# Three moves in the expert stage of a state-space and mixture-of-experts layer: a down product, a block of transposes and the weight loads

## The chip, the cores and the metric

The kernel runs on one core of a Trainium2 chip. The metric is the device time of one execution in microseconds. The core has a matrix engine (TensorE, PE in the profile), a vector engine (VectorE, DVE), an activation engine (ScalarE, ACT), a general engine (GpSimd, POOL) and a queue engine that only issues DMAs here (SyncE, SP). All five run their own instruction streams and meet by semaphores.

## What is computed

A layer with two halves, all in float32. Cut to what matters:

```python
# x: 2 x 1024 tokens of 512
x = x + mamba(layernorm(x))            # projection, conv, selective scan over 1024 steps, gate, projection
h = layernorm(x)
flat = rmsnorm(h) * norm_w             # 2048 x 512
scores = softmax(flat @ router_w.T)    # 32 experts
topk_w, topk_ids = top_k(scores, 4);  topk_w /= sum(topk_w)
for each expert e, its tokens xs:      # 8192 token-expert pairs, ragged
    g, u = split(xs @ w1[e])           # 512 -> 256 + 256
    ys   = (silu(g) * u) @ w2[e]       # 256 -> 512
    routed[token] += topk_w * ys
shared = (silu(flat @ sg) * (flat @ su)) @ sd
out = x + h + routed + shared
```

## The kernel before

It has two blocks of instruction streams, one behind the other; all engines pass from the first to the second together.

The first block (`front`) holds the state-space half, and a closing part with the norms, the router and the shared expert. In the closing the shared expert's down product of a tile of 128 tokens (`dn`, L1510, eight matmul records a tile) goes into one of two banks in turn, and DVE adds the bank to the tile's `base` (`add`, L1024); SP stores it. So the product of tile 14 needs the bank that the addition of tile 12 sets free. The last four tiles, 12 to 15, come at the very end. On DVE the rows of the first expert unit are turned between the last multiplication and the additions of tiles 12 to 15 (L1270 to L1274). The gathers of the first four slots (two units) were issued by POOL as soon as the slot list was known (L1406).

The second block (`experts`) works through units. A slot is 128 rows gathered for one expert; a unit is the two slots of one expert, or a single mixed slot that three experts share (the third unit in each of the first five groups of five). There are 37 units (`NU`), 25 in groups of five and 12 behind them, and 69 slots. The weights of four experts lie in a ring (`RING`), each "place" with 1 MB of gate and up weights (`w1r`) and 0.5 MB of down weights (`w2r`). For a unit u:

- POOL gathers its rows (`gather`, L1686), into one of three row buffers, once the unit three before it is turned; it scatters the finished rows into the output with an addition (`scatter`, L1699). Scatters of one expert are a batch; a batch may be issued only when the batch before it has landed (L1702). In POOL's stream the gather of unit u+4 stands ahead of the scatters of unit u.
- DVE turns the rows into `xT` (`rows_turned`, L1809; one of two buffers; 16 transposes, L171), takes the shares (`shares_of`), and multiplies silu(gate) by up (`mult`, L1815). Its stream is turned(u+2), mult(u+1), turned(u+3), ...
- PE makes the gate product (`gate`, L1897), the up product (`up`, L1907) and the down product (`down`, L1922) in the order gate(u+1), up(u+1), down(u).
- ACT applies silu to the gate product (`silu_gate`, L1768) and copies the down product, weighted with the share, to `y` (`weighted`, L1782, L1787).
- SP loads the next expert's weights into a place (L1664 to L1671): both loads once the last down product that reads the place is done (`y_done`). The gate product waits until both have landed (L1884).

Semaphore `xT_ready` counts the units turned in this block, all but the first; gathers and gate products wait for it by unit number.

Of the kernel before, what the change touches and what calls it, by code (L numbers as in the profile page):

```python
# [44 lines left out]
RING = 4  # L45
# [9 lines left out]
EARLY = 4  # L55
# [48 lines left out]
def front(nc, c, dram):  # L104

    ctx = ExitStack()
    with ctx:
# [93 lines left out]
        order_i, place = inside("order_i", [P, E], I32), inside("place", [P, E])  # L201
# [209 lines left out]
        with nc.Block(no_gpsimd_drain=True) as block:  # L411
# [461 lines left out]
            def _(eng):  # L873
# [390 lines left out]
                for u in range(1, UNITS):  # L1264
# [2 lines left out]
                            add(i)  # L1267
                    mult(u)
                    route(u - 1)
                for v in (0, 1):  # L1270
                    eng.wait_ge(c.gathered[v], 16)
                c.turned(eng, 0, 2)
                for i in range(UNITS - HC, UNITS):
                    add(i)  # L1274

# [281 lines left out]
def experts(nc, c, dram):  # L1557

    ctx = ExitStack()
    with ctx:  # L1560
# [34 lines left out]
        def last_slot(place):  # L1595

            m, v = divmod(place, RING)
            return m * SLOTS + (1, MIXED, 6, 8)[v] if m < SHARED else JOINT + 2 * (place - SHARED * RING) + 1
# [12 lines left out]

        NU = SHARED * (RING + 1) + E - SHARED * RING

        def single(u):
            return len(slots_of(u)) == 1

# [12 lines left out]
        def rows_landed(eng, u):  # L1629

            for n, b, v in row_buffers(u):
                eng.wait_ge(gathered[2 * b + v], 16 * sum(v < len(slots_of(w)) for w in range(b, u + 1, AHEAD // 2)))
# [17 lines left out]
        def after(eng, sem, value):  # L1650
            if value > 0:
                eng.wait_ge(sem, value)
# [9 lines left out]
        with nc.Block(no_gpsimd_drain=True) as block:  # L1662
            @block.sync
            def _(eng):  # L1664
                for place in range(RING, E):
                    u = place % RING
                    at = eng.value_load(c.expert_at[0:1, place:place + 1], min_val=0, max_val=E - 1)
                    ds = bass.ds(at, 1)
                    eng.wait_ge(S["y_done"], last_slot(place - RING) + 1)
                    eng.dma_start(c.w1r[:, u], dram.w1[ds].rearrange("a p k n -> (a p) k n")).then_inc(c.w_landed[u], 16)  # L1670
                    eng.dma_start(c.w2r[:, u], dram.w2[ds].rearrange("a p k n -> (a p) k n")).then_inc(c.w_landed[u], 16)  # L1671

                def one_more(r):
                    eng.wait_ge(S["y_done"], MAIN)
                    eng.wait_ge(R["y_done"], r + 1)
                    for v in range(2):
                        ds = bass.ds(eng.value_load(c.rest_at[0:1, bass.ds(r * 2 + v, 1)], min_val=0, max_val=E - 1), 1)
                        eng.dma_start(c.w1r[:, v], dram.w1[ds].rearrange("a p k n -> (a p) k n")).then_inc(R["w_landed"], 16)
                        eng.dma_start(c.w2r[:, v], dram.w2[ds].rearrange("a p k n -> (a p) k n")).then_inc(R["w_landed"], 16)
                rest(eng, one_more)  # L1680

            @block.gpsimd
            def _(eng):
                eng.sem_inc(R["sent"], 1)

                def gather(u):  # L1686

                    if u >= NU:
                        return
                    if u >= AHEAD // 2:  # L1690
                        old = u - AHEAD // 2
                        after(eng, S["xT_ready"], old)
                        eng.wait_ge(S["share_ready"], shares(last_of(old)))
                    for n, b, v in row_buffers(u):
                        eng.indirect_dma_start(out=xg[:, b, v, :], out_offset=None, in_=dram.flat,  # L1695
                                               in_offset=bass.IndirectOffsetOnAxis(ap=c.slot_token[:, n:n + 1], axis=0))\
                            .then_inc(gathered[2 * b + v], 16)
# [49 lines left out]
                def one_more(r):  # L1747
                    all_landed(eng)
                    eng.wait_ge(R["which_ready"], r * 2 + 2)
                    eng.wait_ge(S["xT_ready"], NU - 1)  # L1750
                    eng.wait_ge(S["share_ready"], shares(MAIN - 1))
                    passed(r, 0)
                    eng.indirect_dma_start(out=xg[:, 0, 0, :], out_offset=None, in_=dram.flat,
                                           in_offset=bass.IndirectOffsetOnAxis(ap=which[:, 0:1], axis=0)).then_inc(R["gathered"], 16)
                    eng.wait_ge(R["y_ready"], r + 1)
                    for v in range(2):
                        at = (which, into_upper)[v][0:PART, 0:1]
                        passed(r, 1 + v)
                        eng.indirect_dma_start(out=dram.out_rows, out_offset=bass.IndirectOffsetOnAxis(ap=at, axis=0),
                                               in_=y[halves[v], 0, :], in_offset=None, compute_op=ALU.add).then_inc(R["added"], 16)  # L1760
                        eng.wait_ge(R["added"], r * 32 + 16 * (v + 1))
                    passed(r, 3)
# [4 lines left out]
            def _(eng):  # L1767
# [14 lines left out]
                def weighted(n):  # L1782
                    eng.wait_ge(S["y_done"], n + 1)
                    eng.wait_ge(S["share_ready"], shares(n))
                    if n >= KEPT:
                        landed(eng, batch_of(n - KEPT))
                    eng.activation(y[:, n % KEPT, :], y_ps[n % 2][:], ACT.Copy, scale=share[:, n % SHARES:n % SHARES + 1])\  # L1787
                        .then_inc(S["y_ready"], 1)

                silu_gate(0)  # L1790
                for u in range(NU):
                    if u + 1 < NU:
                        silu_gate(u + 1)
                    if single(u):
                        act_turned(u)
                    for n in slots_of(u):
                        weighted(n)

                def one_more(r):
                    eng.wait_ge(R["h_done"], r + 1)  # L1800
# [7 lines left out]
            def _(eng):  # L1808
                def rows_turned(u):  # L1809
                    after(eng, S["up_done"], u - 1)  # L1810
                    rows_landed(eng, u)
                    c.turned(eng, u, len(slots_of(u))).then_inc(S["xT_ready"], 1)
                    shares_of(u)
# [18 lines left out]
                            eng.tensor_scalar(to[part, :], xg[part, b, v, bass.ds(at + (DM - 1), 1)], 0.0, None, ALU.add)\  # L1832
                                .then_inc(S["share_ready"], 1)

                rows_landed(eng, 0)
                shares_of(0)
                rows_turned(1)
                mult(0)
                for u in range(NU):
                    if u + 2 < NU:  # L1840
# [25 lines left out]
            def _(eng):  # L1866
# [15 lines left out]
                def ready_for(u):  # L1882
                    for place in places(slots_of(u)[0]):
                        eng.wait_ge(c.w_landed[place % RING], 32 * (place // RING + 1))  # L1884
                    after(eng, S["xT_ready"], u)
                    after(eng, S["act_ready"], u - 1)

                def inner(u, out, first):
# [49 lines left out]

                gate(0)
                up(0)  # L1940
                for u in range(NU):
                    if u + 1 < NU:
                        gate(u + 1)
                    if single(u):
                        turn_act(u)
                    if u + 1 < NU:
                        up(u + 1)
                    down(u)

                def one_more(r):  # L1950
                    eng.wait_ge(R["xT_ready"], r + 1)
# [95 lines left out]
```

## Time and profile before

| | us |
|---|---|
| three runs | 1613.62, 1617.28, 1618.94 |
| their median | 1617.28 |
| the profiled execution, time | 1620.9 |
| its span | 1618.9 |
| PE busy, share of the span | 1449.8, 90% |
| DVE busy | 1308.3, 81% |
| POOL busy | 1077.6, 67% |
| ACT busy | 741.5, 46% |

The expert block begins at about 1231 us and takes the last 388 us. PE is busy all through it, with a granted clock at full rate but for short stretches. The profile is read here by its views: the page (its parts are busy time, slices, queues, the chain that ended last, groups of instructions and DMA issues), the waits (who waited for whom), the timeline of each engine (start, duration, line, operation, output and inputs, count, and in brackets the idle time before and what ended it), and windows (busy time of each engine, granted clock and DMA share in a stretch). Times are from the start of the span.

### The profile page before, as it was taken

The numbers are of one execution on the slowest core, as the hardware profiler recorded it, in microseconds if no ns is written. First come the engines' busy times: TensorE is split into PE (matmuls) and PEld (weight loads), VectorE is DVE, ScalarE is ACT, GpSimd is POOL, SyncE is SP. The second block draws the span as 40 slices with busy tenths as digits, with TensorE's granted clock in tenths as the row PEclk, the third lists the DMA queues.
The fourth block names the chain that finished last, engine by engine and source line by source line (L and its number), as shares of the span: only waits on it lengthen the run. The fifth ranks groups of instructions, "written<-read, shape, count | busy, mean of one in ns | idle before, by whom it ended". The sixth has DMA issues, their size and how long they took to land. (4 is left out here: it accounts for less than half of the span.)

```text
span 1618.9 us, 14732 instructions
## 1 busy us (share of the span) xinstructions
PE 1449.8 (90%) x4412; PEld 725.0 (45%) x4413; DVE 1308.3 (81%) x1931; ACT 741.5 (46%) x1160; POOL 1077.6 (67%) x545
## 2 busy tenths in 40 slices
PE   6578998889998889998798878899998999999996
PEld 3233443334443334443343323444445766667774
DVE  4599999999999999999999997355636777777772
ACT  4566665776656776657566664421000111111111
POOL 0199898999887999989999997230011455555453
PEclk9889999899999999999899999999999999999998
DMA  4540112410113411103310004021412888888895
GB/s 131 221 174 9 42 48 101 179 40 30 35 47 108 171 41 36 35 15 126 129 36 21 28 1 156 20 104 33 182 54 64 225 237 225 218 239 223 259 260 68
DMA packets 63823, 176.86 MB, mean 109 GB/s; under 512 B 10304, under 2 KB 15168, under 8 KB 55040
## 3 DMA queue, kind: packets, MB, share of 16 engines
q1 hardware_dynamic: 48128, 138.59, 24.8%
q0 software_dynamic: 15616, 37.32, 11.1%
q8 instruction: 37, 0.61, 0.2%
q14 instruction: 42, 0.34, 0.1%
HBM read 142.98 MB, written 32.85 MB: 109 GB/s over the span
## 5 line engine op out<-in xcount | busy, mean ns | idle before, releaser
L1342 POOL TENSOR_TENSOR h<-h,c_rep 128x2048 f32<-128x2048 f32 x128 | 579.3, 4530 | 31.2 <-DVE h L945 26.1
L1542 PE MATMUL bank<-h,ident 128*128 128x512 f32 x916 | 449.3, 634 | 93.0 <-POOL h L1342 74.2
L717 ACT ACTIVATE bank<-delta,a_neg 128x512 f32<-128x512 f32 x512 | 335.8, 682 | 178.9 <-DVE h L945 178.1
L1542 PEld LDWEIGHTS bank<-h,ident 128*128 128x128 f32 x916 | 180.6, 202 | 335.9 <-issue 210.9
L945 DVE TENSOR_TENSOR_SCAN h<-bank,state,h 128x512 f32<-128x512 f32 x256 | 306.0, 1260 | 0.5 <-ACT bank L717 0.5
L945 DVE TENSOR_TENSOR_SCAN h<-bank,h 128x512 f32<-128x512 f32 x256 | 290.7, 1199 | 2.8 <-ACT bank L717 2.6
L171 DVE STREAM_TRANSPOSE xT<-xg 32x256 f32<-32x256 f32 (+1 forms) x592 | 247.3, 418 | 56.0 <-DMA xg<-flat,slot_token 48.3
L935 DVE TENSOR_TENSOR h<-bank,b_rep 128x2048 f32<-128x2048 f32 (+1 forms) x105 | 227.5, 2184 | 35.7 <-ACT bank L708 24.2
L1703 POOL DMA_INDIRECT out<-y,slot_token x64 | 101.8, 1590 | 110.1 <-DMA out<-y,slot_token 65.2
L1329 POOL TENSOR_TENSOR h<-du,b_rep 128x2048 f32<-128x2048 f32 (+1 forms) x32 | 125.4, 3920 | 11.5 <-PE bank L1542 11.5
L1787 ACT ACTIVATE y<-y_ps,share 128x512 f32<-128x512 f32 x69 | 47.4, 687 | 185.3 <-PE y_ps L1935 152.3
L1439 PE MATMUL bank<-xnT,w_in 128*128 128x512 f32 x256 | 120.4, 616 | 10.1 <-ACT zs L680 9.2
L1893 PE MATMUL g_ps<-xT,w_ring 128*128 128x256 f32 x512 | 119.4, 387 | 8.2 <-issue 4.3
L1471 PE MATMUL bank<-xnT,w_res 128*128 128x512 f32 x256 | 118.6, 607 | 0.1
L1461 PE MATMUL bank<-w_out,xs 128*128 128x512 f32 x256 | 115.6, 594 | 1.5 <-DVE xs L955 0.9
L1893 PEld LDWEIGHTS g_ps<-xT,w_ring 128*128 128x128 f32 x512 | 98.9, 194 | 38.1 <-issue 25.6
L1893 PE MATMUL u_ps<-xT,w_ring 128*128 128x256 f32 x512 | 115.7, 379 | 0.0
L1935 PE MATMUL y_ps<-w_ring,act 128*128 128x512 f32 x256 | 115.4, 594 | 0.0
L1893 PEld LDWEIGHTS u_ps<-xT,w_ring 128*128 128x128 f32 x512 | 96.9, 190 | 13.0
L1695 POOL DMA_INDIRECT xg<-flat,slot_token x65 | 64.9, 998 | 50.9 <-POOLq L411 25.6
L1407 POOL DMA_INDIRECT xg<-flat,slot_token x4 | 4.0, 1012 | 135.4 <-DVE slot_token L1210 134.5
L1439 PEld LDWEIGHTS bank<-xnT,w_in 128*128 128x128 f32 x256 | 49.9, 197 | 76.6 <-issue 62.4
(238 smaller groups left out, 1530.0 us busy)
## 6 DMA issues: line engine op xcount, KB each, us to landing
w_ring<-in_w SPq DMA_DIRECT2D x32, 1024.0 KB, 5.3
b_rep<-bcd SPq DMA_DIRECT2D x16, 1024.0 KB, 6.9
c_rep<-bcd SPq DMA_DIRECT2D x16, 1024.0 KB, 5.0
w_ring<-in_w SPq DMA_DIRECT2D x32, 512.0 KB, 7.4
w_in<-in_w_in_x SPq DMA_DIRECT2D x32, 256.0 KB, 2.6
w_res<-in_w_in_res SPq DMA_DIRECT2D x32, 256.0 KB, 2.6
xa<-in_x SPq DMA_DIRECT2D x20, 256.0 KB, 3.0
xb<-in_x SPq DMA_DIRECT2D x16, 256.0 KB, 3.0
```

The lines of the kernel that those rows point to most:

```text
L171: ins = eng.transpose(out[cols:cols + PIECE, 0:slots, :, rows:rows + PIECE], x[rows:rows + PIECE, :, :, cols:cols + PIECE])
L717: eng.activation(da[j][:], delta[:, g % 2], ACT.Exp, scale=a_neg[:, col:col + 1])\
L935: eng.tensor_tensor(h[:, q, a:b], du_ps[:].unsqueeze(1).to_broadcast([P, b - a, SEG]), b_rep[:, Q * q + a:Q * q + b, :], ALU.mult).then_in ...
L945: eng.tensor_tensor_scan(h[:, q, j, :], da[j][:], h[:, q, j, :], init, ALU.mult, ALU.add)\
L1329: eng.tensor_tensor(h[:, q, a:b], du[:].unsqueeze(1).to_broadcast([P, b - a, SEG]), b_rep[:, Q * q + a:Q * q + b, :], ALU.mult).then_inc(S ...
L1342: ins = eng.tensor_tensor(h[:, q], h[:, q], c_rep[:, Q * q:Q * q + Q, :], ALU.mult)
L1439: ins = eng.matmul(out[:], w_in[:, n % 2, k, :], xnT[:, s % 2, k, :], start=(k == 0), stop=(k == KC - 1))
L1461: eng.matmul(out[:], xs[:, s % 2, d, i * P:(i + 1) * P], w_out[:, d, :], start=(d == 0), stop=False)
L1471: ins = eng.matmul(out[:], w_res[:, i % 2, k, :], xnT[:, s % 2, k, :], start=(k == 0), stop=(k == KC - 1))
L1542: ins = eng.matmul(y_ps[:], c.ident[:], h[:, q, j, :], start=False, stop=(q == NQ - 1 and j == Q - 1))
L1893: ins = eng.matmul(out[:, f * 2 * P:(f + 1) * 2 * P], c.w1r[:, own, k, first + f * P:first + (f + 1) * P], xT[:, u % 2, k, :], start=(k == ...
L1935: ins = eng.matmul(y_ps[i][:], turned[:, k, v * P:(v + 1) * P], c.w2r[:, places(n)[0] % RING, k, :], start=(k == 0), stop=(k == FC - 1))
```

## The change

Three moves, with no instruction more or less:

1. DVE turns the rows of the second unit in the closing too, behind those of the first and ahead of the additions of tiles 12 to 15. In the expert block it only takes that unit's shares. `xT_ready` counts one unit fewer, so every wait for it asks for one less.
2. SP's load of the gate and up weights of a place waits for the up product of the unit that last used the place, and no longer for its down product. The load of the down weights waits as before and now stands behind it on SP.
3. The last but one unit's down product comes ahead of the last unit's gate product on PE, and on ACT the last unit's silu comes behind the weighted copies of the unit before it.

```diff
@@ front, vector engine, closing
-                for v in (0, 1):
-                    eng.wait_ge(c.gathered[v], 16)
-                c.turned(eng, 0, 2)
+                for u in (0, 1):
+                    for v in (0, 1):
+                        eng.wait_ge(c.gathered[2 * u + v], 16)
+                    c.turned(eng, u, 2)
                 for i in range(UNITS - HC, UNITS):
                     add(i)
@@ experts
+        def unit_of(n):
+            return next(u for u in range(NU) if n in slots_of(u))
@@ sync engine
+                    eng.wait_ge(S["up_done"], unit_of(last_slot(place - RING)) + 1)
+                    eng.dma_start(c.w1r[:, u], dram.w1[ds].rearrange("a p k n -> (a p) k n")).then_inc(c.w_landed[u], 16)
                     eng.wait_ge(S["y_done"], last_slot(place - RING) + 1)
-                    eng.dma_start(c.w1r[:, u], dram.w1[ds].rearrange("a p k n -> (a p) k n")).then_inc(c.w_landed[u], 16)
                     eng.dma_start(c.w2r[:, u], dram.w2[ds].rearrange("a p k n -> (a p) k n")).then_inc(c.w_landed[u], 16)
@@ gpsimd, gather
-                        after(eng, S["xT_ready"], old)
+                        after(eng, S["xT_ready"], old - 1)
@@ scalar engine
-                    if u + 1 < NU:
+                    if u < NU - 2:
                         silu_gate(u + 1)
                     if single(u):
                         act_turned(u)
                     for n in slots_of(u):
                         weighted(n)
+                    if u == NU - 2:
+                        silu_gate(u + 1)
@@ vector engine, start of the experts
-                rows_landed(eng, 0)
-                shares_of(0)
-                rows_turned(1)
+                for u in range(EARLY // 2):
+                    rows_landed(eng, u)
+                    shares_of(u)
                 mult(0)
@@ tensor engine, ready_for
-                    after(eng, S["xT_ready"], u)
+                    after(eng, S["xT_ready"], u - 1)
@@ tensor engine
                 gate(0)
                 up(0)
-                for u in range(NU):
-                    if u + 1 < NU:
-                        gate(u + 1)
+                for u in range(NU - 2):
+                    gate(u + 1)
                     if single(u):
                         turn_act(u)
-                    if u + 1 < NU:
-                        up(u + 1)
+                    up(u + 1)
                     down(u)
+                down(NU - 2)
+                gate(NU - 1)
+                up(NU - 1)
+                down(NU - 1)
```

## Rows read from the trace of the kernel before

**Rows 1.** Waits from 1230 us on: total, times, longest (us).
```profile
POOL out L1703 <- DMA out<-y,slot_token: 65.2, 16, 5.6
```

**Rows 2.** Timeline of PE: end of the closing, first products of the experts.
```profile
1214.97 7.11 PE L1510 MATMUL bank<-w_sd,act_shared 128*128 128x512 f32 x16 [0.93 <-DVE act_shared L1019]
1222.67 7.13 PE L1510 MATMUL bank<-w_sd,act_shared 128*128 128x512 f32 x16 [0.59 <-DVE base L1024]
1231.63 3.69 PE L1893 MATMUL g_ps<-xT,w_ring 128*128 128x256 f32 x16 [1.82 <-PEq L411]
...
1240.79 5.38 PE L1893 MATMUL g_ps<-xT,w_ring 128*128 128x256 f32 x16 [2.02 <-DVE xT L171]
```

**Rows 3.** Timeline of DVE: end of the closing.
```profile
1214.75 7.17 DVE L171 STREAM_TRANSPOSE xT<-xg 32x256 f32<-32x256 f32 x16
1221.93 1.28 DVE L1024 TENSOR_TENSOR base<-base,bank 128x512 f32<-128x512 f32 x2
...
1233.46 7.18 DVE L171 STREAM_TRANSPOSE xT<-xg 32x256 f32<-32x256 f32 x16
```

**Rows 4.** Window: busy time by engine, then granted clock, DMA share, GB/s.
```profile
1242.00:1244.00 2.00, 2.00 (x6) 1.56 (x6) 1.91 (x8) 0.00 (x0) 1.57 (x2) 0.50 0.29 52
```

**Rows 5.** Timeline of PE: matmuls behind a longer wait, in the state-space half.
```profile
297.74 6.07 PE L1542 MATMUL bank<-h,ident 128*128 128x512 f32 x8 [4.46 <-POOL h L1342]
```

**Rows 6.** Timeline of PE: the three gate products with idle time before them.
```profile
1317.25 3.69 PE L1893 MATMUL g_ps<-xT,w_ring 128*128 128x256 f32 x16 [0.61 <-issue]
...
1365.80 3.69 PE L1893 MATMUL g_ps<-xT,w_ring 128*128 128x256 f32 x16 [1.11 <-issue]
...
1415.85 5.11 PE L1893 MATMUL g_ps<-xT,w_ring 128*128 128x256 f32 x16 [2.60 <-issue]
```

**Rows 7.** Timeline of DVE: rows turned behind a gather.
```profile
1408.56 7.18 DVE L171 STREAM_TRANSPOSE xT<-xg 32x256 f32<-32x256 f32 x16 [4.38 <-DMA xg<-flat,slot_token]
...
1507.74 7.18 DVE L171 STREAM_TRANSPOSE xT<-xg 32x256 f32<-32x256 f32 x16 [3.42 <-DMA xg<-flat,slot_token]
```

**Rows 8.** Chain that ended last, in order of time: start, duration.
```profile
1516.60 3.45 PE g_ps L1893 x16
```

**Rows 9.** Timeline of SP: weight loads issued (L1670 1 MB, L1671 0.5 MB).
```profile
1397.23 0.33 SPq L1670 DMA_DIRECT2D w_ring<-in_w  x1
1397.75 0.33 SPq L1671 DMA_DIRECT2D w_ring<-in_w  x1
...
1568.47 0.33 SPq L1670 DMA_DIRECT2D w_ring<-in_w  x1
```

**Rows 10.** Timeline of POOL: scatters issued.
```profile
1270.27 1.49 POOL L1713 DMA_INDIRECT out<-y,slot_token  x1 [0.89 <-ACT y L1787]
...
1538.98 1.62 POOL L1703 DMA_INDIRECT out<-y,slot_token  x1 [5.76 <-ACT y L1787]
...
1570.41 1.57 POOL L1703 DMA_INDIRECT out<-y,slot_token  x1 [0.30 <-issue]
...
1579.03 1.62 POOL L1703 DMA_INDIRECT out<-y,slot_token  x1 [4.44 <-DMA out<-y,slot_token]
1580.96 1.58 POOL L1703 DMA_INDIRECT out<-y,slot_token  x1 [0.30 <-issue]
1587.23 1.56 POOL L1703 DMA_INDIRECT out<-y,slot_token  x1 [4.69 <-DMA out<-y,slot_token]
...
1611.24 1.56 POOL L1703 DMA_INDIRECT out<-y,slot_token  x1 [4.81 <-DMA out<-y,slot_token]
```

**Rows 11.** Timeline of ACT: weighted copies that finish the rows of slots 4, 51, 59 and 68.
```profile
1269.31 0.69 ACT L1787 ACTIVATE y<-y_ps,share 128x512 f32<-128x512 f32 x1 [4.69 <-PE y_ps L1879]
...
1525.26 0.69 ACT L1787 ACTIVATE y<-y_ps,share 128x512 f32<-128x512 f32 x1 [4.57 <-PE y_ps L1935]
...
1566.62 0.69 ACT L1787 ACTIVATE y<-y_ps,share 128x512 f32<-128x512 f32 x1 [4.57 <-PE y_ps L1935]
...
1602.79 0.69 ACT L1787 ACTIVATE y<-y_ps,share 128x512 f32<-128x512 f32 x1 [1.03 <-PE y_ps L1935]
```

**Rows 12.** The page's DMA issues: KB each, median us from issue to landing.
```profile
w_ring<-in_w SPq DMA_DIRECT2D x32, 1024.0 KB, 5.3
```

More of the change, by code:

```diff
@@ L1749, in one_more @@
                     eng.wait_ge(R["which_ready"], r * 2 + 2)
-                    eng.wait_ge(S["xT_ready"], NU - 1)
+                    eng.wait_ge(S["xT_ready"], NU - 2)
                     eng.wait_ge(S["share_ready"], shares(MAIN - 1))
```

## The prediction

> **What bounds the kernel now.** The page's chain that ended last names TensorE and a little DMA, and that misleads; so I read the waits, then the timelines of GpSimd (POOL), TensorE (PE), VectorE (DVE) and ScalarE (ACT) side by side. In the expert part (from 1231 us) POOL's largest wait is for its own scatter-adds to land, 65.2 us [rows 1]: a pair of scatters may start only when the batch before it has landed. Pairing each scatter with the ACT instruction that makes its rows gives its lag behind them. The one of slot 4 starts 0.27 us after its rows are ready (1269.31 + 0.69 = 1270.0 against 1270.27) [rows 10, 11]: there PE sets the pace. After that no scatter waits for its rows. Slot 59's are ready at 1567.31 and goes at 1579.03, 11.7 us later [rows 10, 11], and the last pair goes at 1611.24, though its second half was ready at 1603.5. So the tail is a chain of landings, PE is finished some 15 us before the end, and work taken off PE in the tail is worth nothing by itself.
>
> PE is nevertheless paced by the same chain and paces it. The gather of unit u+5 is issued behind the scatters of unit u; unit 29's rows arrive so that DVE begins to turn them at 1507.74 after 3.42 us of waiting, ends at 1514.92, and its gate product begins at 1516.60 [rows 7, 8]: 1.7 us of room. Where the room is missing PE stops: 0.61, 1.11 and 2.60 us, after the third of which the gate product took 5.11 us for 3.69 [rows 6]. These three, 4.32 + 1.42 = 5.7 us, are each the unit two behind a single-slot unit, and in each DVE waited for a gather, the longest 4.38 us [rows 7]. Over the last units the lag doesn't grow: 13.0 us at slot 51 (ready at 1525.95, scattered at 1538.98), 11.7 at slot 59 [rows 10, 11], while PE makes a unit in 10.34 us ((1566.62 - 1525.26) / 4). I take that as the two being locked together by the weight loads that PE's progress releases.
>
> **Part 1, the second unit's rows turned in the closing.** It adds one block of 16 transposes, 7.18 us, on DVE behind unit 0's and ahead of the last four additions (L1273), and takes it out of the experts' start, with its count in the semaphore. The gathers it needs were issued in one burst with those of unit 0 (L1406), and the rows of unit 0 were turned from 1214.75 without a wait [rows 3], so no DMA is late. But queued behind it on DVE is the addition of tile 12, which frees the bank that the product of tile 14 writes: that product already waits 0.59 us for DVE, until 1222.67 [rows 2]. Unit 0's turning ends at 1221.93 [rows 3], so the addition would start at 1229.1 and the product at 1229.85: 7.18 us later. PE is then idle from 1222.08 for 7.8 us. The trace shows what follows such a wait: after 2.02 us of idling the granted clock was 0.50 from 1242 to 1244 (the 1.2 GHz level) and the gate product took 5.38 us for 3.69 [rows 2, 4], 1.7 us lost; after 4.46 us eight matmuls took 6.07 us for about 3.56 (half of the 7.11 for sixteen), 2.5 us lost [rows 2, 5]. I take 2.0 for the products of tiles 14 and 15, between 1.7 and 2.5. All engines pass from one block to the next together, after the last addition, so the first gate product moves from 1231.63 to about 1240.8.
>
> In return PE loses its wait before the second gate product, 2.02 us, and the low clock behind it, 5.38 - 3.69 = 1.69 us [rows 2]. Net at PE from there on: 7.18 + 2.0 - 2.02 - 1.69 = **+5.5 us** (5.2 to 6.0). DVE has no new lateness: the third unit (one slot) is turned after the first product of unit 0 as before, and VectorE was ahead by the same amount. POOL's gathers of units 2 to 4 and the last store of the base, which POOL waits for, move with the block. Scatter 0 and the scatter at 1270.27 wait for rows from PE, so the chain of landings moves by the same 5.5 us.
>
> **Part 2, gate and up weights behind the up product.** SP now asks for the 1 MB of place p after the up product of the unit that used it last, and for its 0.5 MB of down weights after the down product, as before. A gate product waits for both loads, so its own due time isn't relaxed, and I see no wait of PE for weights in the trace to remove: the loads have three units, some 31 us, in hand. On SP's queue the new wait for the up product stands behind the old wait of the place before. In most units that up product is already done, so the instant at which 1.5 MB is released stays, with the pair now being down weights of p and gate/up weights of p+1. Only where the next user is the single-slot unit does it move: of the 1.5 MB asked for at 1397.23 and 1397.75 [rows 9] and its like, only 0.5 MB goes then, and 1 MB some 3.6 us later, after the product of the single-slot unit. Exactly there the gathers that stop PE are in flight. A load of 1 MB takes 5.3 us to land [rows 12]; 1 MB out of the way of scatters and gathers should bring those gathers forward. The price comes from the tail: from 1580.96 to 1587.23, with no weights and no gathers, a landing let POOL go on after 6.27 us; from 1570.41 to 1579.03, with 1.5 MB and one unit's gathers (0.56 MB), after 8.62 us [rows 10]. That is 2.35 us for 2.06 MB, 1.1 us per MB on the chain; a single gather can gain more, up to the 5.3 us of a whole load, and I take 2.5, nearer the price measured on the chain. With 2.5 us the first two stops vanish, and the third shrinks to under 2 us without a low clock. PE would then lead by some 4 us, but unit 29 has room for only 1.7 and the chain has to gain the rest. I take **-3.0 us** (0 to -5.7).
>
> At the end the shift takes 1 MB out of the last loaded stretch (1568.47 asks for 1.5 MB, afterwards for 0.5 [rows 9]). From 8.62 against 6.27 that is worth 1.1 us pro rata and 2.35 at most [rows 10]: **-1.5 us**. At the front the first load is asked for some 5 us sooner, beside gathers with over 5 us of room: nothing.
>
> **Part 3, the last unit but one's down product ahead of the last gate.** Its rows come 6.9 us sooner, but its scatter waits for the landing before it, not for them. The last unit's down product loses its cover: it must now wait for its own silu and multiplication, 0.69 us of ACT or DVE each, so about 1 us later. The last rows were ready at 1603.48, 9.6 us before POOL used them [rows 10, 11]. Both are nothing; if the cover of the chain were gone, the loss would be that 1 us. On ACT the last silu now stands behind the two weighted copies, which are done before the gate product ends.
>
> **Sum.** +5.5 - 3.0 - 1.5 = +1.0 us. The profiled execution had a span of 1618.9 us and took 1620.9; it would take 1621.9. It lies 3.6 us above the median of the three runs, 1617.28, so the time to expect is **1618.3 us**.
>
> **The rivals.** *A, the loads only change places.* For: DMA is busy nearly throughout this stage, the chain of landings runs by itself from 1270 to 1506, and what leaves one landing falls on the next. Against: PE's stops are single gathers, which do have a neighbour to gain from. The sum is then +5.5 - 1.5 = +4.0, 1621.3 us (up to 1622.8 if the tail gives nothing). The Trainium skill speaks for it: "DMA: Bandwidth & Descriptors", section "Issuing engines are not separate DMA queues", says that transfers started by any engine run on the same 16 DMA engines and interleave. By that rule the sum is A's; the trace agrees in that the landing with weights beside it took 2.35 us longer, and doesn't show whether a load moved by 3.6 us gains anything.
>
> *B, slower: the low clock is paid twice.* PE idles 1.82 us before the first gate product [rows 2], without a fall now because it was busy before; behind a stretch at half rate it may fall again. That is 1.7 us more, and with A +5.5 + 1.7 - 1.5 = +5.7: 1623.0 us. It decides from a half-rate gate product at 1241 on.
>
> *C, full relief.* All three stops go (-5.7), the chain gains by it, and the tail gives 2.35: +5.5 - 5.7 - 2.35 = -2.5, 1614.7 us; with another 3 us if each of the four groups' landings shortens by 0.8, 1611.7.
>
> *D, the closing doesn't hold.* If the product of tile 14 weren't waiting for tile 12's addition, part 1 would bring -3.7 in place of +5.5: -8.2, 1609.1 us. The 0.59 us in [rows 2] is against it.
>
> **How the numbers follow.** My forecast (1615 to 1621) has 0.42, A 0.22, B 0.12, C 0.16, D 0.08. A measurement of this kernel can tell about 0.3%, 4.85 us, from no change. Slower than that is B and a part of A and of the forecast's upper end: 0.21. Faster is D and C's lower part: 0.13. The rest, 0.66, is within. The range from 1611.5 to 1623.0 takes in A, C and half of B and leaves out D.
>
> **What would show it.** In the trace after: 32 transposes in a row on DVE before the four additions; PE waiting 7 to 8 us for "DVE base" before the product of tile 14, with a granted clock of 0.50 behind it; no wait between the first up product and the second gate product; the stops at the three gate products shorter than 0.61, 1.11 and 2.60, or gone; lags of POOL again near 11.6 in the last units; the stretch between the last loaded landing and its next scatter near 7.1 in place of 8.62. The forecast is wrong if the wait in the closing is short, if a single gate product near 1241 runs at half rate, or if PE's stops come back elsewhere, above all at units 25 to 30.

## The result, and the profile after

The changed kernel took 1625.26 us (median of six executions, 1622.98 to 1630.87) beside 1616.53 us for the kernel before (six, 1613.62 to 1618.94): a ratio of 1.0058, 95% interval 1.0035 to 1.0081. It is slower by 8.7 us where +1.0 was forecast and 1618.3 us, at most 1623.0, was expected. A repeat on another occasion (e8, below) gave 1.0028 (1.0011 to 1.0045), 1623.6 beside 1617.72. The change costs some 4 to 9 us. Three single executions behind the ratios below (1745.19, 2825.2 and 8484.88 us) ran in a slower state, and every ratio is taken without them.

The profiled execution of after took 1624.15 us with a span of 1622.1. The page's first part:

```profile
PE 1448.7 (89%) x4412; PEld 722.0 (45%) x4413; DVE 1308.8 (81%) x1931; ACT 741.8 (46%) x1160; POOL 1077.1 (66%) x545
```

No engine does other work than before; busy times say nothing here. The end of the closing does. Timeline of PE of after (start, duration, line, operation, count, and in brackets the idle time before and what ended it), beside [rows 2]:

```profile
1217.17 7.11 PE L1511 MATMUL bank<-w_sd,act_shared 128*128 128x512 f32 x16 [0.93 <-DVE act_shared L1019]
1232.06 9.46 PE L1511 MATMUL bank<-w_sd,act_shared 128*128 128x512 f32 x16 [7.79 <-DVE base L1024]
1243.35 3.69 PE L1900 MATMUL g_ps<-xT,w_ring 128*128 128x256 f32 x16 [1.82 <-PEq L411]
1246.88 3.62 PE L1900 MATMUL u_ps<-xT,w_ring 128*128 128x256 f32 x16
1250.33 3.62 PE L1900 MATMUL g_ps<-xT,w_ring 128*128 128x256 f32 x16
```

And of DVE, beside [rows 3]:

```profile
1216.94 14.37 DVE L171 STREAM_TRANSPOSE xT<-xg 32x256 f32<-32x256 f32 x32
1231.32 1.28 DVE L1024 TENSOR_TENSOR base<-base,bank 128x512 f32<-128x512 f32 x2
```

The product of tile 14 waits 7.79 us (0.59 before) for the addition of tile 12, which stands behind 14.37 us of transposes, and then takes 9.46 us for 7.13. In return the second gate product at 1250.33 waits for nothing and takes 3.62 us; before it waited 2.02 and took 5.38. Granted clock behind the wait (windows of after: stretch, its length, then busy time of the engines, granted clock, DMA share, GB/s):

```profile
1233.00:1235.00 2.00, 2.00 (x4) 0.89 (x3) 0.00 (x0) 0.00 (x0) 0.00 (x0) 0.50 0.64 240
1237.00:1239.00 2.00, 2.00 (x6) 0.95 (x5) 0.69 (x1) 0.00 (x0) 0.00 (x0) 1.00 0.00 0
```

At 1233 to 1235 the clock is 0.50, the 1.2 GHz level, and at 1237 it is back at 2.4 GHz: 9.46 - 7.13 = 2.33 us lost.

Of the three places where PE stopped [rows 6] only the second still has a stop; a new one, smaller, stands one group further on (PE of after, gate products with 0.4 us or more of idle time before them, up to 1500 us):

```profile
1363.92 3.69 PE L1900 MATMUL g_ps<-xT,w_ring 128*128 128x256 f32 x16 [0.86 <-issue]
...
1459.45 3.69 PE L1900 MATMUL g_ps<-xT,w_ring 128*128 128x256 f32 x16 [0.49 <-issue]
```

So PE's stops, 4.32 us and another 1.42 of low clock before, are 1.35 us. That is the relief that was forecast, and yet the kernel is slower. POOL's scatters at the end of after, beside [rows 10]:

```profile
1575.02 1.61 POOL L1708 DMA_INDIRECT out<-y,slot_token  x1 [5.47 <-DMA out<-y,slot_token]
1576.94 1.57 POOL L1708 DMA_INDIRECT out<-y,slot_token  x1 [0.30 <-issue]
1583.18 1.62 POOL L1708 DMA_INDIRECT out<-y,slot_token  x1 [2.06 <-DMA out<-y,slot_token]
...
1614.74 1.56 POOL L1708 DMA_INDIRECT out<-y,slot_token  x1 [4.20 <-DMA out<-y,slot_token]
```

From 1576.94 to 1583.18, the stretch from slot 58 to slot 59, a landing took 6.24 us; before, with 1.5 MB and gathers beside it, the same stretch took 8.62 [rows 10]. The stretch ahead of it, 1565.36 to 1575.02, took 9.66, where it was 1568.50 - 1560.23 = 8.27 before. The chain of landings is the last thing again: the last weighted copy ends at 1608.44 + 0.69 = 1609.13, and the last pair of scatters goes 5.6 us later.

A way to compare any two traces: cut each at the start of the product of tile 12 (F), at the first scatter (s0), at the scatter of slot 45, and at the end.

| us | F | F to s0 | s0 to slot 45 | slot 45 to end | time |
|---|---|---|---|---|---|
| before | 1214.97 | 37.37 | 253.67 | 112.89 | 1620.90 |
| after | 1217.17 | 42.95 | 251.47 | 110.56 | 1624.15 |

(The last stretch is cut at the end of the span; what lies around the span is 2.0 us in both.) From F to s0 after is 5.58 us longer. F itself lies 2.2 us later though nothing ahead of it was changed: over all profiles below it lies anywhere from 1212.1 to 1218.5. This pair of profiles differs by 3.3 us, the medians by 8.7. With 2 to 5 us (standard deviation) from one execution to the next, one pair of profiles can't show where 5 us went; that had to come from timed runs and from many profiles together.

### The profile page after: what moved, and what is told of

Read it like the earlier page. It is cut to its first block and busy times, and to the rows that moved or that the text cites. A ratio compares the mean times of both kernels' runs of the same rounds, so it can differ in the third digit from the quotient of the medians.

```text
span 1622.1 us, 14732 instructions
## 1 busy us (share of the span) xinstructions
PE 1448.7 (89%) x4412; PEld 722.0 (45%) x4413; DVE 1308.8 (81%) x1931; ACT 741.8 (46%) x1160; POOL 1077.1 (66%) x545
## 5 line engine op out<-in xcount | busy, mean ns | idle before, releaser
L1708 POOL DMA_INDIRECT out<-y,slot_token x64 | 101.7, 1589 | 102.8 <-DMA out<-y,slot_token 61.5
L1440 PE MATMUL bank<-xnT,w_in 128*128 128x512 f32 x256 | 116.8, 601 | 11.7 <-ACT zs L680 10.8
L1780 ACT ACTIVATE act<-g_ps 128x512 f32<-128x512 f32 (+1 forms) x37 | 21.0, 568 | 140.8 <-PE g_ps L1900 86.6
```

## The experiments

Theory T: part 1 costs some 5.5 us at the first scatter, all of which reaches the end; part 2's relief of PE is given back further on. Rival R1: part 1 costs less at the end than at the start and part 2 is the culprit. Rival R2: part 3 costs. Each ratio is to the kernel before in the same session, with its 95% interval.

### One part at a time, and two

Part 1 alone (its three hunks of the diff), part 2 alone (SP), part 3 alone (the loops of PE and ACT):

> Part 1 alone (second unit's rows turned in the closing, ahead of the additions). Theory one, the whole loss is the closing: the product of tile 14 waits 7.2 us longer and runs its first microseconds at the low clock, the second gate product no longer waits, net +5.5 us at the first rows and +6 to +9 us at the end. Theory two, the loss beyond the closing is the weight loads': +3 to +5.5 us, well below the 8.7 us of all three parts.

> Part 2 alone (gate and up weights behind the up product). Theory one: -2 to -4.5 us (PE's stops behind the single-slot units shrink, the last loaded landing is shorter by 1 to 2.3 us). Theory two, loads in a worse phase against the scatters: +2 to +4 us. Theory A of the prediction, loads only change places: -1.5 to 0.

> Part 3 alone (last but one down product ahead of the last gate product). Both theories: 0, within 1 us; PE's last product ends about 1 us later and the last scatters start where they did. If the median moves by over 3 us, the landings in the tail depend on PE in a way that neither theory has.

Pairs of parts, and the whole change again:

> Parts 1 and 2 without part 3. If the parts add up as measured one by one (+6.8, -1.6 and -2.6 us), +5 us. If the early weight loads cost where PE has lost its pauses (the loads then start earlier against the scatters), +9 us, as all three parts together.

> Parts 1 and 3 without part 2. Additive: +4 us. If the interaction sits between parts 1 and 3 rather than with the weight loads, +9 us.

> The changed kernel with part 1 taken back. If part 1 is the loss: -4 to -1 us against the kernel before. If parts 2 and 3 lose by something that part 1 doesn't cause: +2 us or more.

> The changed kernel itself once more, on the chip of the three above. The first measurement stands at +9.4 us (5.7 to 13.1). If the parts simply add up it comes down to +3 to +6; if there is an interaction it stays near +9.

Repeats, with the kernel before as its own control:

> The kernel before under another name. Ratio 1.000 within the interval. Its profile adds a second one without any part: first scatter 37.4 us behind the closing's start; if part 2 slows the chain, slot 45 is scattered some 250 us behind the first scatter and the lag there is under 12 us; if not, this profile looks like those with part 2 (253 us, lag 12 to 14).

> Part 2 alone once more. Theory one, the early loads slow the chain of landings in the groups (253.4 us from the first scatter to that of slot 45 against 249.4, six profiles each) and give 1.4 us back in the tail: slot 45 near 253 us, lag over 12 there, stops behind the single-slot units under 1.3 us each, ratio 0.999 to 1.002. Theory two, the difference of the profiles is chance: slot 45 near 250 us, lag 5 to 11, ratio 0.996 to 0.999.

> Part 1 alone once more; the four kernels with it stand at +4.5 to +7.6 us, its own first measurement at +6.8 (2.8 to 11). If the end follows the first scatter: +5.6. If something beyond the closing costs too: +8.

| run | parts | ratio | interval | us, before |
|---|---|---|---|---|
| e13 | none | 1.0005 | 0.9986-1.0024 | 1618.59, 1619.18 |
| e1 | 1 | 1.0042 | 1.0017-1.0068 | 1623.99, 1617.91 |
| e15 | 1 | 1.0036 | 1.0015-1.0057 | 1624.25, 1619.18 |
| e2 | 2 | 0.9990 | 0.9970-1.0011 | 1617.87, 1617.91 |
| e14 | 2 | 1.0016 | 0.9996-1.0037 | 1619.18, 1619.18 |
| e3 | 3 | 0.9984 | 0.9960-1.0008 | 1618.78, 1617.91 |
| e5 | 1, 2 | 1.0033 | 1.0015-1.0051 | 1623.66, 1617.72 |
| e6 | 1, 3 | 1.0047 | 1.0024-1.0070 | 1623.90, 1617.72 |
| e7 | 2, 3 | 0.9996 | 0.9975-1.0017 | 1618.58, 1617.72 |
| e8 | 1, 2, 3 | 1.0028 | 1.0011-1.0045 | 1623.60, 1617.72 |

Every kernel of this table with part 1 is slower, and none without it. Four contrasts, each with and without part 1 and the rest alike (e1 and e15 against e13; e5 against e2 and e14; e6 against e3; after and e8 against e7), give 0.34, 0.30, 0.63 and 0.47%: about 0.43%, 7 us, give or take 2. The same for part 2 (e2 and e14 against e13; e5 against e1 and e15; e7 against e3; after and e8 against e6) gives -0.02, -0.06, +0.12 and -0.04%: nothing, give or take 2 us again. For part 3 (e3 against e13, e7 against e2 and e14, e6 against e1 and e15, after and e8 against e5) they are -0.21, -0.07, +0.08 and +0.10%: nothing. So R1 and R2 fall. Part 2, which was to bring 4.5 us, brings none.

### How much of the start reaches the end

e4 does part 1 with the second block of transposes two additions later:

```diff
                 c.turned(eng, 0, 2)
-                for i in range(UNITS - HC, UNITS):
+                for i in range(UNITS - HC, UNITS - HC + 2):
+                    add(i)
+                for v in (2, 3):
+                    eng.wait_ge(c.gathered[v], 16)
+                c.turned(eng, 1, 2)
+                for i in range(UNITS - HC + 2, UNITS):
                     add(i)
```

> Part 1 with the second block of transposes behind the additions of tiles 12 and 13 and ahead of those of tiles 14 and 15. Theory one: the product of tile 14 starts as in the kernel before, the block ends 1 to 1.5 us later, the second gate product doesn't wait, net -2 to -3 us at the first rows. If part 1's loss is something else than the held bank, this loses as well, +3 us or more.

It gave 1.0003 (0.9984 to 1.0023). PE of e4: tile 14 has its old wait, and the block delays the last additions instead, so that PE idles 4.65 us ahead of the experts, and the first gate product runs at the low clock:

```profile
1220.82 7.13 PE L1515 MATMUL bank<-w_sd,act_shared 128*128 128x512 f32 x16 [0.59 <-DVE base L1024]
...
1232.60 5.38 PE L1898 MATMUL g_ps<-xT,w_ring 128*128 128x256 f32 x16 [4.65 <-PEq L411]
...
1241.27 3.62 PE L1898 MATMUL g_ps<-xT,w_ring 128*128 128x256 f32 x16
```

F to s0 is 37.93 us, 0.56 more than before, where after has 5.58 more. The expectation of 2 to 3 us less had left out that idle time and the low clock behind it.

e9 is the kernel before with unit 1's rows turned once more in the closing and nothing taken out of the experts: part 1's cost without its return.

```diff
                 c.turned(eng, 0, 2)
+                for v in (2, 3):
+                    eng.wait_ge(c.gathered[v], 16)
+                c.turned(eng, 1, 2)
                 for i in range(UNITS - HC, UNITS):
```

> The kernel before with the second unit's rows turned in the closing as in part 1, and turned again in the experts as before: what part 1 adds, without what it takes away. The closing then costs 7.2 us of waiting and 2.0 to 2.4 us at the low clock, and the wait before the second gate product stays: first scatter +9.3 us behind the closing's start. Theory one (the end follows the first scatter): +9 us at the end. Theory two (part 1's loss has another source than the closing, since the profiles show only +1 to +2 us at the end): well off +9.

It gave 1.0051 (1.0031 to 1.0071), 1626.8 us. PE of e9 shows both costs, the wait in the closing and the wait in the experts:

```profile
1229.88 9.44 PE L1513 MATMUL bank<-w_sd,act_shared 128*128 128x512 f32 x16 [7.79 <-DVE base L1024]
...
1250.31 5.38 PE L1896 MATMUL g_ps<-xT,w_ring 128*128 128x256 f32 x16 [2.01 <-DVE xT L171]
```

F to s0 is 46.87, 9.50 us more than before. The six profiles with part 1 in its first place put the first scatter 5.5 to 6.0 us later. So shifts of the first scatter by +0.6, +5.6 and +9.5 us went with times of +0.5 (e4; -2.6 to +3.7), about +7 (part 1; 5 to 9) and +8.3 (e9; 5 to 11.5) us. The end follows the first scatter by its whole shift, within what these runs resolve.

The late place with the other parts:

> All three parts, with the second block of transposes behind the additions of tiles 12 and 13. The product of tile 14 no longer waits. First scatter +0.6 us behind the closing's start (profile of part 1 in this place), against +5.6 in the changed kernel: 5 us faster than the changed kernel, 0 to -4 us against the kernel before. If the interaction of the parts, and not the closing, is the loss, it stays at +4 or more.

> The late place of part 1 (behind the additions of tiles 12 and 13) with part 3 and without part 2: first scatter +0.6 us behind the closing's start, the loads as before, the last but one rows earlier for executions in which TensorE ends last. -3 to 0 us against the kernel before; the best candidate of the study. If part 1's place isn't what matters: +3 or more.

e12 (late place and parts 2, 3) gave 1.0013 (0.9994 to 1.0032), e16 (late place and part 3) 0.9988 (0.9967 to 1.0009). With the wait in the closing gone, what is left of the change is no difference. It is not a gain either, though up to 4 us had been expected of e12.

### What the loads and the scatters cost

e10 leaves out all weight loads in the experts (units after the fourth expert compute with old weights), e11 all scatters of routed rows (the routed part is missing from the output). Both are read for time alone.

> The kernel before without the 28 pairs of weight loads in the expert stage: units 5 on work with the weights of the first four experts, so the output isn't the reference's. If the landings are slowed by the loads (1.1 us per MB by the prediction), the chain of scatters catches up with TensorE, TensorE's stops behind the single-slot units vanish, and the end comes at TensorE's pace plus one landing: -12 to -17 us. If the loads only fill gaps of the DMA engines: 0 to -3.

> The kernel before without the scatters of the experts' rows: the routed half of the output is missing. The end is then TensorE's last product and one copy: its stops vanish if gathers were late because they stood behind scatters. Expected -4 to -6 us at TensorE's end for the stops, and the 15 us behind TensorE's last product go: -19 to -22 us. If the stops have another source, -15.

e10 gave 0.9935 (0.9912 to 0.9958), 1609.3 us; e11 0.9872 (0.9844 to 0.9900), 1598.99 us. e10 gained less than the 12 to 17 us expected. Without loads POOL waits more for rows than for landings (waits of e10, from 1260 us on: total, times, longest):

```profile
POOL out L1703 <- ACT y L1787: 69.4, 22, 6.9
...
POOL out L1703 <- DMA out<-y,slot_token: 14.0, 6, 4.5
```

The same of after, with its full-slot scatters at L1708:

```profile
POOL out L1708 <- DMA out<-y,slot_token: 61.5, 17, 5.5
...
POOL out L1708 <- ACT y L1792: 23.8, 8, 9.9
```

The name behind the arrow needs a check here. In e10 all but two of the scatters put down to ACT do start within 0.5 us of the end of their weighted copy. In after only the longest of the eight does, the first scatter's 9.9 us; the seven others start 7.2 to 12.7 us behind theirs, so it wasn't their rows that they waited for. The scatters of slots 45 and 59 go 0.28 us after their rows in e10, and PE stops nowhere behind the second gate product. Its 9.6 us are about all that a placing of the loads could bring to this kernel, and part 2 was forecast to bring half of them. Without scatters, e11 is 20 us faster: its last copy ends at 1597.05 and the span at 1597.6, so no chain of landings stands behind PE's last unit.

In e10's profile s0 to slot 45 takes 237.0 us against 253.67 before. Of these 16.7 us, 10.8 are the scatter's lag behind its rows (11.08 us before, 0.28 in e10); the rows themselves come 5.9 us later with loads, about what the three stops and their low clock make (5.7). So POOL loses time to the loads all along, and PE in its stops.

### Where part 2's relief goes

The sixteen profiles of kernels that compute the whole layer, e17 and e18 aside, fall in two heaps. With part 2 (after, e2, e5, e7, e8, e12, e14) s0 to slot 45 takes 253.6 us on average (249.4 to 259.3); without it (before, e1, e3, e4, e6, e9, e13, e15, e16) 248.8 (244.5 to 253.7): 4.8 us longer, with heaps that overlap. From slot 45 to the end it is 111.8 against 113.0: 1.25 us shorter.

The 4.8 us are too much to lay on part 2. PE isn't slower: slot 45's rows are ready 240.9 us behind the first scatter with part 2 and 240.7 without, and the whole difference is the scatter's lag behind them. That lag is 10.0 to 14.0 us in all seven with part 2, 10.0 to 11.1 in five without it, and 4.7 to 5.2 in four (e6, e9, e15, e16). Against the five of the like kind (251.3 us on average) part 2's heap is 2.4 us longer. And the profiled executions are not the medians of their kernels: with part 2 they were 1.0 us slower on average, without it 1.9 faster. The timed contrasts, nothing give or take 2 us, are the firmer figure.

PE's stops of 0.4 us and more in the groups, added up, are 1.35 to 2.61 us in six of the seven profiles with part 2 (5.55 in e12), against 2.07 to 4.64 without it: 2.6 against 3.4 on average. So they shrank a little. But in e2, e8 and e12, where slot 45 was scattered 13.3 us or more behind its rows, PE stopped later, on entering the two-slot stretch. PE of e2, and the block of transposes on DVE that it waited for:

```profile
1508.97 6.36 PE L1897 MATMUL g_ps<-xT,w_ring 128*128 128x256 f32 x16 [4.24 <-issue]
```

```profile
1501.70 7.18 DVE L171 STREAM_TRANSPOSE xT<-xg 32x256 f32<-32x256 f32 x16 [9.36 <-DMA xg<-flat,slot_token]
```

These are the rows of unit 28. DVE waited 9.36 us for their gather, which stands in POOL's stream behind the last piece of a single slot, and that piece waits for the landing of the third batch (below). PE had stood for 4.24 us when the block ended, with a low clock behind it (6.36 us for 3.69). e8 shows 4.42 us, e12 6.71 and e14, with a lag of 13.1 us, 1.65 at the same place. What PE had won it stood there and gave back.

The batches of scatters show why. A group of five units has four batches: the first unit's two slots; the second unit's two and a piece of the single slot; the second piece (`slot_upper`) with the fourth unit's slots; the third (`slot_last`) with the fifth unit's. Time from a batch's first scatter to the next one's, added over groups 1 to 4, means over the heaps:

| us | 1st | 2nd | 3rd | 4th |
|---|---|---|---|---|
| without part 2 | 38.68 | 57.18 | 46.24 | 55.16 |
| of these, the five with a like lag | 37.44 | 57.39 | 46.25 | 58.67 |
| with part 2 | 34.08 | 56.21 | 49.93 | 59.46 |
| e17 | 36.38 | 57.61 | 45.29 | 56.61 |
| e18 | 36.73 | 54.81 | 46.22 | 60.20 |

Against the five of the like kind the first batch, which lost the 1 MB, is 3.4 us shorter, the second 1.2 shorter, the third 3.7 longer and the fourth 0.8 longer; in sum nothing (199.7 and 199.8 us). The 2.4 us stand in the first group, where the piece of slot 4 waits for its rows (1270.27 us before, 1270.31 in e2), so that a shorter batch ahead of it brings nothing. Only in the third do the heaps not overlap: 47.7 to 52.0 us with part 2, 45.8 to 47.1 in all nine without. The load beside it was there before, too. What differs is when its two halves are asked for. SP of before, then of e2, behind the same down product:

```profile
1279.95 0.34 SPq L1670 DMA_DIRECT2D w_ring<-in_w  x1
1280.47 0.33 SPq L1671 DMA_DIRECT2D w_ring<-in_w  x1
```

```profile
1279.98 0.33 SPq L1675 DMA_DIRECT2D w_ring<-in_w  x1
1281.10 0.34 SPq L1673 DMA_DIRECT2D w_ring<-in_w  x1
```

Before, 1 MB and 0.52 us later 0.5 MB; with part 2, 0.5 MB and, 1.12 us later, the next place's 1 MB, since SP first reads the next expert's number between the two. The landing behind it, POOL of before and of e2:

```profile
1278.77 1.36 POOL L1713 DMA_INDIRECT out<-y,slot_upper  x1 [7.01 <-DMA out<-y,slot_token]
...
1291.25 1.33 POOL L1713 DMA_INDIRECT out<-y,slot_last  x1 [6.03 <-ACT y L1787]
```

```profile
1278.81 1.36 POOL L1717 DMA_INDIRECT out<-y,slot_upper  x1 [7.01 <-DMA out<-y,slot_token]
...
1292.84 1.33 POOL L1717 DMA_INDIRECT out<-y,slot_last  x1 [7.59 <-DMA out<-y,slot_token]
```

From the piece at 1270.3 us on the two traces are alike up to here. All four pieces belong to slot 4, whose rows were ready at 1270.0 us, so each waited for a landing, also where the profile names ACT. From `slot_upper` to `slot_last` it is 12.48 us before and 14.03 in e2: with the loads in that order and at that distance the landing came 1.55 us later. (One pair alone doesn't show it: e4 and e15, which lack part 2, have 13.95 and 13.69 us at this place. The sums over four groups, with no overlap, do.) Two kernels take order and distance apart. e17 is the kernel before with its two `dma_start` lines swapped: 0.5 MB first, distance 0.5 us. e18 is part 2 with the next expert's number read ahead of the wait, which brings the distance down to 0.5 us:

```diff
+                expert = lambda place: eng.value_load(c.expert_at[0:1, place:place + 1], min_val=0, max_val=E - 1)
+                ahead = expert(RING)
...
-                    ds = bass.ds(at, 1)
+                    ds = bass.ds(ahead, 1)
                     eng.wait_ge(S["up_done"], unit_of(last_slot(place - RING)) + 1)
...
+                    if place + 1 < E:
+                        ahead = expert(place + 1)
                     eng.wait_ge(S["y_done"], last_slot(place - RING) + 1)
```

> The kernel before with only the order of the two loads of a place swapped: down weights (0.5 MB) first, gate and up weights (1 MB) 0.5 us behind, both after the down product. In part 2 the pair stands in this order too, with the 1 MB 1.1 us later than the 0.5 MB. Batches from piece 4.1 to 4.2 and from 4.2 to slot 9 take 13.8 and 14.0 us with part 2, 12.3 and 12.5 without (seven and nine profiles). Theory order: they take 13 us or more here too, and slot 45 comes 251 to 255 us behind the first scatter. Theory lateness (what counts is the 0.6 us that part 2's register load and second wait put between the two): about 12.3 and 12.5, slot 45 at 246 to 251.

> Part 2 with the next expert's number loaded ahead of the wait for the down product, so that the 1 MB load follows the 0.5 MB load as closely as SP can issue it. Theory lateness: the two batches fall back from 13.8 and 14.0 to about 12.5 and 13, slot 45 at 247 to 251 us, end 2 to 4 us sooner than part 2 alone (ratio 0.996 to 0.999). Theory order, or any other: as part 2, slot 45 at 251 to 255, ratio 0.999 to 1.002.

e17 gave 0.9986 (0.9967 to 1.0005), 1616.18 us: the order alone costs nothing, and its third batch (45.29) is as without part 2. e18 gave **0.9967 (0.9949 to 0.9986), 1612.42 us beside 1618.81**, the fastest here that computes the whole layer and 6.4 us faster than the kernel before. Its interval lies below that of e14 (0.9996 to 1.0037) and overlaps those of e2 and e17. It was timed once, in twelve executions. SP of e18:

```profile
1277.33 0.34 SPq L1678 DMA_DIRECT2D w_ring<-in_w  x1
1277.87 0.33 SPq L1674 DMA_DIRECT2D w_ring<-in_w  x1
```

So part 2 as written gains at the first batch and loses at the third. By e2 and e14 against e18 the distance of 0.6 us between two loads is worth some 0.36%, 6 us, give or take 4. How that works inside the queues isn't shown. The batches of e18 bear it out in the third (46.22, among those without part 2); its fourth (60.20) is that of the kind with a long lag, which it is (11.5 us at slot 45). In its first group it doesn't come out, POOL of e18:

```profile
1274.49 1.36 POOL L1720 DMA_INDIRECT out<-y,slot_upper  x1 [5.39 <-DMA out<-y,slot_token]
...
1288.69 1.33 POOL L1720 DMA_INDIRECT out<-y,slot_last  x1 [7.75 <-ACT y L1794]
```

That is 14.20 us, no less than e2's 14.03, and again a wait for a landing whatever the name. Besides, F to s0 is 35.67 us in this profile and 37.36 in those of e2 and e14, because the second gate product kept the full clock; the edit doesn't touch the work of PE or DVE there, so that 1.7 us of this execution's gain can't be laid on it. How often that happened in the other eleven isn't on record. The account by batches rests on one profile each of e17 and e18, and e18 with the late place or part 3 was not run.

## Why the prediction was wrong

**Part 1, the wait: right.** A wait of 7.8 us was foreseen for the product of tile 14, and 7.79 was measured; 2.0 us for the low clock, 2.33 measured; the second gate product without wait at 3.62 us, as said. Net +5.58 for +5.5. That the shift reaches the end whole was argued from the chain of landings; e4, e9 and part 1 show it: +0.5, +8.3 and about +7 us for shifts of 0.6, 9.5 and 5.6. The 7 is above 5.6 within its uncertainty. The covered queues (gathers, base store, third unit) cost nothing that the runs show.

**Part 2, -3.0 us: wrong, and this is the step that failed.** The text took the three stops and what a landing gains from 1 MB less beside it, and let PE's gain of about 4 us become 3 at the end. Right in it: the stops shrank (4.32 to 1.35 us in after, 3.4 to 2.6 on average), the first batch got shorter, and the room where the two-slot stretch begins limits PE: stops came there, at unit 28 and not 29, in the four profiles whose lag at slot 45 was 13.1 to 14.0 us, and in none whose lag was 12.7 or less. Wrong: that "the instant at which 1.5 MB is released stays" everywhere else. The distance between its two halves moved from 0.5 to 1.1 us, which looked like nothing, and the third batch got longer (3.7 us over four groups, no overlap) about as much as the first got shorter. By the profiles of the like kind s0 to slot 45 is 2.4 us longer; the timed contrasts say 0, give or take 2, for part 2 with its tail. So nothing came of -4.5. The sign named for this, stops that come back at units 25 to 30, was there in four of seven profiles. The nearest rival was A, that the loads only change places, at +4.0 in all. The Trainium skill's rule under it ("DMA: Bandwidth & Descriptors", section "Issuing engines are not separate DMA queues": all issuers share the 16 engines and their transfers interleave) agrees with the first batch's gain and the third's loss, and says nothing of the distance; A's sum is still below what was measured, 5.9 us in e8 and 8.7 in the result.

**The tail, -1.5 us: right where the lag is long.** From slot 45 to the end it is 1.25 us shorter on average. In the four profiles with part 2 whose lag at slot 59 is 10 us or more (after, e5, e7, e14) the stretch from slot 58 to 59 took 6.0 to 6.2 us, against 8.6 to 9.3 in the five of that kind without it; the stretch ahead of it gave 0.5 back. In the three with a short lag it took 8.0 to 8.8, against 8.7 without part 2; their tail is 1.2 us shorter as well, and where that comes from isn't shown.

**Part 3, nothing: right.** Contrasts between -0.21 and +0.10%. The last unit's down product lost its cover as said, and waited 0.85 us for its own multiplication, PE of after:

```profile
1604.70 3.70 PE L1942 MATMUL y_ps<-w_ring,act 128*128 128x512 f32 x8 [0.85 <-DVE act L1829]
```

ACT's last two copies then follow as before, ahead of POOL's last scatter at 1614.74 by 5.6 us:

```profile
1606.72 0.69 ACT L1792 ACTIVATE y<-y_ps,share 128x512 f32<-128x512 f32 x1 [5.69 <-PE y_ps L1942]
1608.44 0.69 ACT L1792 ACTIVATE y<-y_ps,share 128x512 f32<-128x512 f32 x1 [1.03 <-PE y_ps L1942]
```

**The rivals.** B's time was nearest (1623.0), by another way: its second fall of the clock did not come, the first gate product took 3.69 us after 1.82 idle. C's stops went for the most part, and its gain did not follow. D fell with the 7.79 us.

**The sum.** +5.6 (part 1; about 7 when timed), 0 give or take 2 (part 2 with its tail), 0: +5.6 to +7, against +5.9 and +8.7 measured. The range's upper end of 1623.0 gave the changed kernel no case in which part 1 stands whole and part 2 brings nothing or a loss; that case, +5.5 to +7, was the likeliest once A was taken seriously.

## What to carry to other kernels

A block moved into idle time of its engine is paid by whatever stands behind it in that engine's stream: put it behind the work that another engine waits for (e4 against e1: 0.6 for 5.6 us at the first scatter). A load moved away from one victim in a saturated stage meets the next one; the stage's whole length, not the stop that vanished, is the gain, and running the kernel without the loads shows first how much there is to win (here 9.6 us). When a wait is moved between two DMA issues, look at what else the issuing engine does between them (here a register load, 0.6 us), and try it outside the gap: the one run that did was the fastest.

## What the runs showed of the hardware

- The distance between two weight loads of 0.5 and 1 MB on one queue, 0.5 or 1.1 us, went with 0.9967 (e18) against 0.9990 and 1.0016 (e2, e14) in time.
- The expert stage settles in one of two ways by chance. At slot 59 the scatter lags its rows by 10 to 12.5 us in ten profiles (before, after, e1, e3, e4, e5, e7, e13, e14, e18) and by 1 to 3.5 us in eight (e2, e6, e8, e9, e12, e15, e16, e17), with no values between. The same program falls either way: e2 and e14, after and e8, e1 and e15 are pairs of one kernel. What tips it is not shown for those without a stop of PE. That PE is finished some 15 us before the end held in the profile shown, and not in those eight.
- A wait for several semaphores can carry the wrong name. `slot_last` at 1291.25 us is put down to ACT, yet its rows were ready 21 us earlier.
- The same idle time has not always the same price: after 2.01 us of idling the second gate product took 5.38 us in e9 and 3.69 in e18.
- Single executions have a standard deviation of 2 to 5 us in the kernels that compute the whole layer, and of 0.8 us both without the loads (five executions) and without the scatters (four). So the spread needs both.
